# One Newton chain for the last five tiles of a layer norm, and a reordered head of the scatter queue

## The reference, cut to what matters

```
x = layernorm(x + attention(x))            # 16 heads, elu feature maps
logits = x @ router_w
a = argmax(logits); w = softmax(logits)[a]
hid = gelu(x @ w1[a] + b1[a])              # 128 -> 256
moe = (hid @ w2[a] + b2[a]) * w            # 256 -> 128
out = layernorm(x + moe)                   # (v - mean) / sqrt(var + 1e-5)
```

## Time and profile before

| what | value |
|---|---|
| median of 3 runs | 106.53 us (105.52 to 107.42) |
| the profiled execution's own time | 106.11 us |
| its span | 104.4 us |
| mean granted PE clock | 0.915 |
| busy in the span: PE, DVE, ACT, POOL | 77.7, 65.8, 59.9, 64.0 us |
| the 16 stores (POOL L540) | 15.9 us busy, first at 77.2 us, last at 100.5 us |

### The profile page before, as it was taken

How to read it: one execution, slowest core, us unless ns; L and a number is a source line. 1 busy time by engine, 2 the same in 40 slices (tenths; PEclk the granted TensorE clock), 3 DMA queues, 4 the chain that set the end, 5 groups by cost and what they waited for, 6 DMA issues and landing times.

```text
span 104.4 us, 2202 instructions
## 1 busy us (share of the span) xinstructions
PE 77.7 (74%) x592; PEld 67.1 (64%) x594; DVE 65.8 (63%) x270; ACT 59.9 (57%) x186; POOL 64.0 (61%) x109
## 2 busy tenths in 40 slices
PE   5987999999999698073868599799899999600000
PEld 3765869998887695043557499699798989400000
DVE  4699995746759789881105336535788876878500
ACT  0416697767288999990137447746457695822200
POOL 6758799840005378908767747730286898777670
PEclk9999999999999999975599999999999999995555
DMA  1937999700000001453887788840000101011110
GB/s 38 341 134 227 366 322 291 206 8 3 0 0 9 0 0 51 152 203 92 258 254 224 210 271 230 226 125 2 0 0 25 60 25 50 25 50 53 50 50 25
DMA packets 9674, 12.16 MB, mean 117 GB/s; under 512 B 1426, under 2 KB 7230, under 8 KB 9662
## 3 DMA queue, kind: packets, MB, share of 16 engines
q1 hardware_dynamic: 8276, 9.69, 28.3%
q0 software_dynamic: 1024, 2.11, 8.2%
q10 hardware_dynamic: 362, 0.23, 1.0%
HBM read 6.07 MB, written 2.11 MB: 78 GB/s over the span
## 4 chain that ended last, share of the span: by engine, by line
PE 31%; DVE 23%; DMA 12%; POOL 11%; ACT 10%; issue 9%; POOLq 1%; DVEq 1%
DMA acc<-x_rows,source 8%; PE ps_a L1050 6%; PE ps_o L1050 6%; POOL out L540 6%; PE ps_q L1050 5%; PE ps_k L1050 4%; PE ps_r L1050 4%; DMA x_sb<-L_attn_x 4%; DVE acc L1000 3%; ACT rows L636 3%; POOL rstd L393 3%; DVE st L1032 2%; ACT rows L648 2%; POOL acc L521 2%; PE ps_t L1060 2%
## 5 line engine op out<-in xcount | busy, mean ns | idle before, releaser
L521 POOL DMA_INDIRECT acc<-x_rows,source x16 | 16.2, 1014 | 8.3 <-issue 3.7
L1000 DVE SCALAR_TENSOR_TENSOR acc<-ps_o,share,acc 128x128 f32 x29 | 10.2, 351 | 15.5 <-PE ps_o L1050 8.4
L1050 PE MATMUL ps_o<-w_sb,hid 128*128 x116 | 18.7, 284 | 1.2 <-ACT hid L715 1.0
L540 POOL DMA_INDIRECT out<-k_parts,source x16 | 15.9, 997 | 4.6 <-issue 3.7
L393 POOL TENSOR_TENSOR rstd<-ve,exponent 128x4 f32<-128x4 f32 (+3 forms) x14 | 12.5, 896 | 9.2 <-DVE ve L1038 6.7
L1050 PEld LDWEIGHTS ps_o<-w_sb,hid 128*128 128x128 f32 x116 | 15.2, 191 | 2.2 <-issue 2.0
L715 ACT ACTIVATE hid<-ps_q,shared 128x128 f32<-128x128 f32 x30 | 9.3, 362 | 5.6 <-PE ps_q L1050 5.6
L720 ACT ACTIVATE k_parts<-acc,shift,rstd 128x128 f32<-128x128 f32 x15 | 7.0, 488 | 8.8 <-DVE shift L1022 8.8
L715 ACT ACTIVATE hid<-ps_k,shared 128x128 f32<-128x128 f32 x28 | 8.7, 363 | 5.4 <-PE ps_k L1050 4.3
L1050 PE MATMUL ps_q<-xs_t,shared 128*128 (+1 forms) x60 | 10.5, 298 | 0.4 <-ACT xs_t L710 0.4
L1050 PE MATMUL ps_k<-xs_t,shared 128*128 x56 | 9.7, 295 | 1.3 <-ACT xs_t L710 1.3
(11 more groups left out here) (210 smaller groups left out, 193.1 us busy)
## 6 DMA issues: line engine op xcount, KB each, us to landing
shared<-w_sb SPq DMA_DIRECT2D x29, 129.0 KB, 2.4
w_sb<-L_ffn_w SPq DMA_DIRECT2D x1, 1792.0 KB, 7.7
x_rows<-rows SPq DMA_DIRECT2D x4, 258.0 KB, 2.1
x_sb<-L_attn_x SPq DMA_DIRECT2D x4, 256.0 KB, 4.2
acc<-x_rows,source POOLq DMA_INDIRECT x16, 3.3
out<-k_parts,source POOLq DMA_INDIRECT x16
wqkv_sb<-L_attn_Wqkv ACTq DMA_DIRECT2D x1, 192.0 KB, 3.9
wo_sb<-L_attn_Wout SPq DMA_DIRECT2D x1, 64.0 KB, 4.7
```

Source lines behind the costliest of these rows:

```text
L521: pool.indirect_dma_start(acc[:, t, :], None, x1_rows, bass.IndirectOffsetOnAxis(ap=source[:, t:t + 1], axis=0), bounds_check=last_token, ...
L540: pool.indirect_dma_start(out_rows, bass.IndirectOffsetOnAxis(ap=source[:, t:t + 1], axis=0), res[:, t, :], None, bounds_check=last_token, ...
L1000: dve.scalar_tensor_tensor(out=tile, in0=ps_y[j % 2], scalar=share[:].rearrange("p t e -> p (t e)")[:, bass.ds(t_of[j] * ROW + j, 1)], in1 ...
L1050: return pe.matmul(o, l, r, start=start, stop=stop)
```

## The change

It does three things. Groups 6 and 7 become one group of five tiles, 11 to 15, with one Newton chain after step 28. POOL's store 0 moves ahead of power 1, and power 1 and power 2 now both stand ahead of store 1. The shifts of groups 1 and 5 move one step back (after step 16 in place of 15, and after 25 in place of 24), and the apply of tile 1 moves one step back on ACT (16 to 17).

```diff
-GROUPS = [(0, 1), (1, 2), (2, 4), (4, 6), (6, 8), (8, 11), (11, 14), (14, 16)]
+GROUPS = [(0, 1), (1, 2), (2, 4), (4, 6), (6, 8), (8, 11), (11, 16)]
 POWERS = 6
-POWER_BEFORE = {0: 1, 1: 2, 3: 3, 4: 4, 6: 5}
-SHIFT_AFTER = {15: 1, 17: 2, 20: 3, 22: 4, 24: 5}
-APPLY_AFTER = {16: [1], 18: [2], 19: [3], 21: [4], 22: [5], 23: [6], 24: [7], 25: [8], 26: [9], 27: [10],
+POWER_BEFORE = {3: 3, 4: 4, 6: 5}
+SHIFT_AFTER = {16: 1, 17: 2, 20: 3, 22: 4, 25: 5}
+APPLY_AFTER = {17: [1], 18: [2], 19: [3], 21: [4], 22: [5], 23: [6], 24: [7], 25: [8], 26: [9], 27: [10],
                28: [11, 12, 13, 14, 15]}
...
             for t in range(NT):
-                if t in POWER_BEFORE:
+                if t == 1:
+                    power_of(1)
+                    power_of(2)
+                elif t in POWER_BEFORE:
                     power_of(POWER_BEFORE[t])
                 store(t)
```

## The result

The changed kernel takes 107.55 us against 106.47 us of the kernel before, medians of 20 runs each. The ratio is 1.0088, with a 95% interval of 1.006 to 1.0115: slower by 0.88%, which is 0.94 us. The ratio leaves out the runs of either kernel that lie over 1.5% above its fastest, among them one of the changed kernel that took 124.87 us at a granted clock of 0.639; the two medians, of all runs, differ by 1.08 us. The prediction was 0.96 us slower and 107.3 us. The difference is under the 2% from which the prediction speaks of slower, so it falls in the case "same", to which it gave 0.82. The profiled execution took 106.80 us with a span of 105.1 us and a granted clock of 0.911.

The account below looks back on a forecast made before the run. POOL's store queue was taken as bound, except 0.31 us of wait for the second chain. Terms 0 + 0 + 0 + 0.96 us gave 107.07 us on the profiled footing, 107.36 on the mean's, stated as 107.3; range 105.7 to 108.2.

Parts of the forecast that it names:

- same: Whole kernel: measured change stays under 2% (2.1 us) of the kernel before; chance 0.82.
- The bound: End of the kernel: POOL's store queue nearly binds; only 0.31 us of the wait for the second chain reach the end.
- The head, shift 1, apply 1: Around powers 1 and 2 on POOL, DVE and ACT: the moves cost 0; for apply 1, -0.23 to 0.60 us.
- gelu 19 late: ACT: apply 1 ahead of gelu 19 delays output 19 and the loop by 0.60 us, 107.67 us; chance 0.15.
- Shift 5: DVE at step 25: shift 5, apply 8, gelus and outputs 27 and 28 all come 0.10 us later.
- One chain: DVE to POOL at the end: add 28 to store 11 takes 4.48 us; the last store comes 0.96 us later.
- The sum: Whole kernel: 0.96 us slower, span 105.36, time 107.07 us on the profiled execution's footing.
- POOL stays the bound: POOL's last stores: they run unbroken and only the old 0.31 us vanish, 105.80 us; chance 0.17.
- DVE sets the end: DVE's last chain: last shift and end both come 2.87 us earlier, 103.24 us; chance 0.04.

Follow-up runs that it names:

- shift 5 alone: Kernel before with only the shift of group 5 moved from after step 24 to after 25, run twice: ratios 0.9956 and 0.9937 to the kernel before.
- two Newton steps: Kernel before with two Newton steps in place of three in both chains: ratio 0.9938; the same edit in the changed kernel: 1.0137.
- the head alone: Kernel before with store 0 ahead of powers 1 and 2, and shift 1 and apply 1 one step back: ratio 1.0019.
- the kernel before, again: Kernel before, unedited, profiled on the same chip as the experiments: ratio 1.003 to the kernel before.
- stores 3 and 4 left out: Changed kernel without the stores of tiles 3 and 4, whose rows are not written: ratio 1.0115 to the kernel before.
- the merged chain alone: Kernel before with only groups 6 and 7 merged into one Newton chain, store queue head and all shifts as before: ratio 1.0194.
- the last experiment: Second run of the kernel before with only the shift of group 5 one step back: ratio 0.9937 to the kernel before.

## Why the prediction was right

**The bound.** POOL's store queue with 0.31 us of wait for the second chain. Confirmed three ways: shift 5 alone gains 0.28 us in the profile where the steps are as in the earlier trace rows, and from there on store 14 has only its issue gap ahead; two Newton steps gain 0.50 us in the profile, the 0.51 us that store 14 waited, and no more; of 1.49 us by which add 24 is late, 0.28 us reach the last store of the kernel before.

**The head, shift 1, apply 1: 0.** Right. Store 0 and power 1 end at 77.92 with 0.71 us left, and the head alone measures 1.0019 with 1 inside. Output 18's wait (0.23) went and one of 0.39 us appeared ahead of output 19: its matmul starts at +1.17 against +1.12. The slack by my count was 0, and 0.05 us was lost, of no effect on power 2's queue. The rival "gelu 19 late" needed 0.60 us; add 20 is at +3.20 against +3.16, so it is refuted.

**Shift 5: 0.10 us later.** Apply 8 came 0.15 us later, add 28 at +12.88 against the +12.83 of the prediction. Right within 0.05.

**One chain: add 28 to store 11, 4.48 us.** Measured 4.53. The Newton steps cost the same on five columns as on two (160 to 170 ns), and the first chain instruction took 0.40 us in place of 0.17, while the one ahead of it took 0.17 in place of 0.38. In this pair of traces the two cancel, and that is luck: in others neither is long, and the way from add 28 to the first store behind the chain is 4.27 us (the kernel before, again) or 4.30 us (stores 3 and 4 left out). So the 4.48 us carry a scatter of 0.2 us that the prediction has no term for. The traces don't say what makes the long ones.

**The sum.** Store 15 is 1.06 us later against power 2, predicted 0.96; the ratio of many runs gives 0.94, the medians 1.08. The profiled execution itself took 106.80 us where the sum says 107.07: power 2 came 0.36 us earlier, and the stretch from there to store 15 was 0.10 us longer than predicted. The sum in short: three more stores behind the chain are 3.83 us, add 28 came 2.82 us earlier, and the way from it to the store grew by 0.05. POOL's idle time ahead of store 11 was predicted at about 1.6 us and is 1.72.

**The rivals.** "POOL stays the bound" would have been 105.80 and "DVE sets the end" 103.24; both are excluded by the measured interval and by the 1.72 us of idle time on POOL. The last shift of DVE did come earlier, 95.08 against 98.22, and the kernel got slower: this is the reading of the chain of waits that the prediction warned of.

What the prediction did not see is how much its own number hangs on the steps' pace. It treats 0.96 us as a property of the kernel. Where add 24 comes 1.4 us later, the same change costs 1.7 to 1.9%, since in the kernel before the 0.78 us of waiting for power 5, itself late in POOL's backlog, give way first, and the changed kernel has neither this wait nor a backlog ahead of store 11. Which of the two counts for more is not separated: the merged chain alone, which keeps the shift of group 5 after step 24, was run on such chips only. A rival should have asked what a late step costs in either kernel.

## What to carry to other kernels

Merging the last groups of a pipeline saves instructions on the engine that makes them, but the first tile of the merged group now waits for the last; if an in-order queue of fixed cost per item drains behind it (here 1.27 us a store), each item that used to overlap the chain now comes behind it. What the earlier start of the chain gives back has to be set against that, here 2.82 us against 3.83 us. Before you shorten the chain that the view of waits ends in, subtract the usual issue gap from the idle time of the engine behind it: what is left (0.31 us here) is all there is to gain. Filling a stall by moving a wait one step back, without the merge, gave that part where it could be read in a profile (0.28 us).

## What the runs showed of the hardware

The same kernel took 106.5 us at first and 106.2 us beside the last experiment, and 111.3 to 111.8 us on three chips in between. Whether the chip makes the difference, or something else that differed between these occasions, was not tested. In the traces of the latter most of the 5 us lie ahead of the layer norm (power 2 starts at 83.78 against 79.00), and two stalls stand out behind it. DVE waits 0.91 us ahead of add 20 and 0.70 us ahead of add 24, in the kernel before, again:

```profile
87.78 0.35 DVE L1000 SCALAR_TENSOR_TENSOR acc<-ps_o,share,acc 128x128 f32 x1 [0.91 <-PE ps_o L1050]
...
93.01 0.35 DVE L1000 SCALAR_TENSOR_TENSOR acc<-ps_o,share,acc 128x128 f32 x1 [0.70 <-PE ps_o L1050]
```

PE had finished both outputs well before: add 20 and add 24 start 1.12 and 1.02 us after the end of their outputs, where in the first profile it was 0.28 and 0.38. The granted clock is 1.00 in both stretches (86 to 88 and 92 to 94 us), as in the first profile from 80 to 82 and 84 to 87. From 86 to 88 the queue of kind "instruction" has a packet, but so it has from 80 to 83 in the first profile, which is about as far behind power 2, with no such stall; and from 91.8 to 93, ahead of add 24, there is none. So a packet there is not enough to make the stall, and what does is open.
